# One signal per tile from TensorE and a hand-written loop, in a kernel that packs the lower triangles of 2,048 Gram matrices

## What is computed

```python
Z = jnp.einsum('bnd,bmd->bnm', inputs, inputs)      # inputs: (2048, 64, 256) float32
li, lj = jnp.tril_indices(64, k=-1)
return Z[:, li, lj]                                 # (2048, 2016) float32
```

## Time and profile before

| | us |
|---|---|
| median of 3 runs (lowest, highest) | 411.94 (411.42, 413.04) |
| the profiled execution's own time | 411.66 |
| its span, from the first to the last instruction | 409.9 |
| PE busy (matmuls) | 378.6 |
| DVE busy | 367.1 |
| ACT busy | 177.5 |
| POOL busy | 197.7 |

### The profile page before, as it was taken

One profiled execution on the slowest core, in us unless ns is written; L12 is line 12 of the kernel. 1 busy time (PEld: TensorE's weight loads), 2 busy tenths in 40 slices (PEclk: granted clock), 3 DMA queues, 4 the chain that ended last, 5 costly groups with the idle time before them and its releaser, 6 DMA issues.

```text
span 409.9 us, 68720 instructions
## 1 busy us (share of the span) xinstructions
PE 378.6 (92%) x33024; PEld 371.8 (91%) x33024; DVE 367.1 (90%) x240; ACT 177.5 (43%) x821; POOL 197.7 (48%) x974
## 2 busy tenths in 40 slices
PE   4589999999999999999999999999999999999950
PEld 4588999999999999999999999999999999999950
DVE  3328999999999999999999999999999999999965
ACT  0101245444455444555444546434555443555184
POOL 1000074663818274472818366381827457281845
PEclk9999999999999999999999999999999999999995
DMA  7259999999999999999999999999999999995407
GB/s 307 66 211 426 423 421 421 421 422 421 418 425 422 423 421 422 421 422 422 420 414 367 423 383 399 406 395 423 383 422 365 421 398 423 404 374 238 119 20 202
DMA packets 21291, 151.01 MB, mean 368 GB/s; under 512 B 2705, under 2 KB 2833, under 8 KB 4881
## 3 DMA queue, kind: packets, MB, share of 16 engines
q1 hardware_dynamic: 18752, 135.77, 82.1%
q10 hardware_dynamic: 2512, 14.97, 9.5%
HBM read 134.22 MB, written 16.52 MB: 368 GB/s over the span
## 4 chain that ended last, share of the span: by engine, by line
PE 88%; issue 4%; DVE 3%; ACTq 2%; ACT 1%; DMA 1%; DVEq 0%
PE bank_set L297 88%; ACTq L154 2%; DMA x_in<-x_dram 1%; DVE packed_rows L147 1%; DVE x_in L248 1%; DVE x_turned L224 1%; ACT products L324 1%; ACT packed_rows L142 1%; ACT packed_rows L136 0%; DVE packed_rows L136 0%; DVE x_turned L253 0%; DVEq L76 0%; DVEq L223 0%; ACTq L315 0%; DVEq L273 0%
## 5 line engine op out<-in xcount | busy, mean ns | idle before, releaser
L297 PE MATMUL bank_set<-x_turned 32*64 32x64 f32 x33024 | 378.6, 236 | 18.0 <-issue 9.1
L297 PEld LDWEIGHTS bank_set<-x_turned 32*64 32x64 f32 x33024 | 371.8, 132 | 24.7 <-issue 20.4
L224 DVE STREAM_TRANSPOSE x_turned<-x_in 128x2048 f32<-128x2048 f32 x128 | 293.1, 2293 | 33.2 <-DMA x_in<-x_dram 21.1
L147 POOL COPY packed_rows<-row_halves 32x32 f32<-32x32 f32 (+30 forms) x930 | 190.1, 204 | 202.1 <-DVE row_halves L241 164.5
L324 ACT COPY products<-bank_set 128x512 f32<-128x512 f32 (+1 forms) x91 | 68.5, 759 | 189.0 <-PE bank_set L297 170.9
L241 DVE STREAM_TRANSPOSE row_halves<-products 128x1024 f32<-128x1024 f32 x60 | 72.2, 1204 | 0.0
L142 ACT COPY packed_rows<-row_halves 128x128 f32<-128x128 f32 x240 | 53.5, 299 | 19.7 <-issue 19.0
L136 ACT COPY packed_rows<-row_halves 128x32 f32<-128x32 f32 (+30 forms) x465 | 60.8, 219 | 0.2 <-DVE row_halves L241 0.2
L324 ACT ACT_TABLE_LOAD x1 | 1.3, 1283 | 17.4 <-PE bank_set L297 17.4
L248 DVE STREAM_TRANSPOSE x_in<-products 128x512 f32<-128x512 f32 (+1 forms) x5 | 4.8, 999 | 4.0 <-ACT products L324 4.0
L147 POOL COPY packed_rows<-x_in 32x32 f32<-32x32 f32 (+30 forms) x31 | 4.9, 209 | 4.4 <-DVE x_in L248 4.4
## 6 DMA issues: line engine op xcount, KB each, us to landing
x_in<-x_dram SPq DMA_DIRECT2D x128, 1024.0 KB, 17.1
y_dram<-packed_rows ACTq DMA_DIRECT2D x21, 504.0 KB, 8.9
y_dram<-packed_rows ACTq DMA_DIRECT2D x7, 252.0 KB
y_dram<-packed_rows ACTq DMA_DIRECT2D x28, 63.0 KB
y_dram<-packed_rows SPq DMA_DIRECT2D x2, 504.0 KB, 4.8
y_dram<-packed_rows SPq DMA_DIRECT2D x1, 380.0 KB
y_dram<-packed_rows ACTq DMA_DIRECT2D x1, 380.0 KB
y_dram<-packed_rows SPq DMA_DIRECT2D x1, 124.0 KB
```

The costliest lines, as they stand in the source:

```text
L147: return copy(packed_rows[first:first + BLOCK, group % 2, :, at + BLOCK:at + i], halves(group)[first + BLOCK:first + HALF, i, :, 0:i - BLOCK])
L224: nc.vector.transpose(x_turned[:, j].rearrange("p c b s (h u n v) -> p u v (c b s h) n", h=ROWS // BLOCK, u=PAIRS, v=PAIR), x_in[:, k]).th ...
L297: done = nc.tensor.matmul(bank_sets[s][side * HALF:(side + 1) * HALF, g, at, :].rearrange("r (n u v) -> r u n v", u=PAIRS, v=PAIR), rows, ...
```

## The change

There are four edits, all about semaphores and PE's loop; no matmul, copy or DMA is added or taken away.

1. Only the last of an input tile's 128 matmuls raises `tile_multiplied[j]`, by one. `ARRAY_TILES` goes away, and the three waits on it (SP's for the late loads, DVE's, ACT's) count tiles instead of array tiles.
2. The loop of PE is written out with a register, `count`, a label, and a branch at the lap's end.
3. The register is raised by 3 in the middle of the lap's last tile (after its first slot) instead of at the lap's end.
4. Since the wait on `kept[0]` in the lap's last tile now comes behind that addition, `kept[0]` starts at 3 like `kept[1]`, and the waits of DVE on `kept[s]` are raised to match.

```diff
-    ARRAY_TILES = QUADRANTS * SIDES
...
-                    sync.wait_ge(tile_multiplied[j], (lap + 1) * ARRAY_TILES)
+                    sync.wait_ge(tile_multiplied[j], lap + 1)
...
-            pool.sem_inc(kept[1], LAP)
+            for s in range(SETS):
+                pool.sem_inc(kept[s], LAP)
...
-                    dve.wait_ge(tile_multiplied[j], lap * ARRAY_TILES)
+                    dve.wait_ge(tile_multiplied[j], lap)
...
-                    dve.wait_ge(kept[s], (lap + 1 + s) * LAP)
+                    dve.wait_ge(kept[s], (lap + 2) * LAP)
...
-            def multiply(j, step):
-
-                pe.wait_ge(turned[j], step)
+
+            count = nc.alloc_register(pe.engine, "count")
+
+            def multiply(j):
+
+                pe.wait_ge(turned[j], count)
                 s, in_set = set_of(j)
                 for slot in range(SLOTS):
                     at = in_set * SLOTS + slot
+                    if j == LAP - 1 and slot == SLOTS - 1:
+                        pe.reg_add(count, count, LAP)
                     for c in range(CHUNKS):
                         if in_set == SET_TILES[s] - 1 and slot == SLOTS - 1 and c == CHUNKS - 2:
 
-                            pe.wait_ge(kept[1 - s], step)
+                            pe.wait_ge(kept[1 - s], count)
...
-                                if c == CHUNKS - 1 and slot == SLOTS - 1:
-                                    done.then_inc(tile_multiplied[j], 1)
-
-            with pe.Fori(LAP, (LAPS + 1) * LAP, LAP) as step:
+
+                done.then_inc(tile_multiplied[j], 1)
+
+            pe.reg_mov(count, LAP)
+            pe.br("lap")
+            with nc.body("lap", valid_engines=[pe.engine]):
                 for j in range(LAP):
-                    multiply(j, step)
+                    multiply(j)
+                pe.br_lt(count, (LAPS + 1) * LAP, on_true="lap", on_false="laps_done")
+            nc.switch_bb("laps_done")
...
-                act.wait_ge(tile_multiplied[j + SET_TILES[s] - 1], (lap + 1) * ARRAY_TILES)
+                act.wait_ge(tile_multiplied[j + SET_TILES[s] - 1], lap + 1)
```

## The result

The changed kernel takes 409.09 us (median of 6 runs, 408.41 to 409.84), the kernel before 412.42 us beside it (6 runs, 411.42 to 413.65). The ratio is 0.9919, with a 95% interval of 0.9896 to 0.9942: 3.3 us faster, where 3.4 us were forecast. By the interval the gain lies between 2.4 and 4.3 us. The profiled execution of the changed kernel took 408.65 us, with a span of 406.9 us against 409.9 us.

What follows compares the result with a forecast made beforehand. PE and the DMA engines were taken to bound the kernel at one pace within 1%. Tile 122 3.1 us earlier, tile 123's end another 0.2, the start about 0.1: 3.4 us off 411.94, so 408.5 us, range 406.4 to 410.6 us.

Steps and rivals of the forecast that it cites:

- two resources at one pace: In mid-kernel a group of eight tiles costs the DMA engines 23.6 us and PE 23.4 us, the same within 1%.
- The signals: At each tile's end inside a lap, one signal for eight saves PE 0.12 us, 0.24 us per lap.
- the met wait in mid-tile: Near the middle tile's end, PE's already met wait on `kept[1]` costs nothing: 84 records, where the ordinary pace gives 85.
- The loop: At PE's lap end only the branch remains; the addition and the move go, 0.065 us less per lap.
- laps between the stores of 8.4 to 8.5 us: Sign to look for in PE's timeline after the change: laps between stores should take 8.4 to 8.5 us.
- DVE would not stop PE: In mid-kernel DVE is busy 8.43 us a lap, just under PE's new 8.475 us.
- The last store's delay: Behind the last delaying store PE begins tile 122 at 374.7 us, between 374.5 and 374.9 us, 3.1 us earlier.
- The tail keeps its length: From tile 123's end ACT is the chain; the tail keeps its length and moves by 3.3 us.
- my first rival: At the end group 13's stores issue faster and PE becomes the chain: 4 to 5 us earlier, about 407 us; chance 0.14.
- The addition in mid-tile: Rival: in the lap's last tile it empties PE's queue, stopping PE 0.35 us per lap: 413.8 us; chance 0.05.
- The second rival: At tile ends, in the loop or in the stores' DMA costs the gain is lost: 410.5 to 412 us; chance 0.17.
- The fourth rival: PE's clock falls to 1.2 GHz in pauses behind stores, adding 28 us: 430 us or more; chance 0.02.

Runs made afterwards that it cites:

- the addition at the end: Changed kernel with the register's addition back at the lap's end, just ahead of the branch: 409.71 us, ratio 0.9938 to the kernel before.
- the single signal alone: Kernel before plus one signal per tile in place of eight, old loop kept: 409.28 us, ratio 0.9920.
- the written-out loop alone: Kernel before plus the written-out loop with the addition in mid-tile, eight signals kept: 410.36 us, ratio 0.9939.
- the two cuts: DVE turns half of each tile from tile 6, groups 0 to 12 store 16 columns: before 411.1 us, whole change 391.8 us.
- small stores and an early load 4: Changed kernel with six stores for groups 0 to 12, two for group 13, load 4 not held back: 415.00 us, ratio 1.0064.
- the early load 4: Changed kernel with load 4 no longer held back until tile 1 is multiplied: 404.71 us, ratio 0.9806 to the kernel before.

## Why the prediction was right, step by step

**The step that carried it: two resources at one pace.** The landing of load 122 at 372.0 us was forecast not to move, and it did not, while PE's own lap fell by half a microsecond. The gain is PE's distance behind the loads, and no more. What the prediction calls the pace of the DMA engines is the pace of the few that are furthest behind. Its 3.7 us for a group's stores is a measured difference and already contains that, so the sum was not harmed.

**The signals.** The share of the tile's end was right (0.14 us counted); what I took off was 0.12 us each, and all of it went, 0.145 us. That the met wait in mid-tile costs nothing was the right ground for it.

**The loop: the term that was mis-sized.** I took off 0.065 us, the recorded 36 and 29 ns. It was 0.17 us. The step that failed is reading a sequencer instruction's record as its cost. At the lap's end each of the two costs 0.08 to 0.10 us. With both terms PE's own lap is 8.28 us, not 8.475 us, so the sign "laps between the stores of 8.4 to 8.5 us" did not come. That the total came out nearly right in spite of it is owed to the cap, which hides PE's pace: 0.2 us a lap over 40 laps is 8 us that never reached the end.

**DVE would not stop PE.** Only just. Three laps of the changed kernel before the loads become the limit take 24.79 us, 8.26 us each (length, busy of PE, PEld, DVE, ACT, POOL, clock, DMA share, GB/s):

```profile
59.78:84.57 24.79, 24.79 (x2311) 24.58 (x2305) 24.79 (x14) 12.47 (x56) 14.94 (x75) 1.00 1.01 421
```

DVE is busy in all of it. Its limit is thus 8.26 us a lap; my 8.43 us, from its busy time before, was too high. A turn behind a wait takes 2.31 us, two turns without one 4.46 us together (both in the timeline below), and in the kernel before more of the turns stood behind a wait. PE and DVE now run side by side at one pace. None of this decided anything, since the loads' pace is 8.83 us.

**The last store's delay.** The forecast was that tile 121 waits and tile 122 follows, at 374.7 us between my two cases. What happened, in the timeline of the changed kernel:

```profile
369.61 2.31 DVE L224 STREAM_TRANSPOSE x_turned<-x_in 128x2048 f32<-128x2048 f32 x1 [1.63 <-DMA x_in<-x_dram]
371.84 1.20 DVE L241 STREAM_TRANSPOSE row_halves<-products 128x1024 f32<-128x1024 f32 x1
371.97 2.95 PE L302 MATMUL bank_set<-x_turned 32*64 32x64 f32 x256 [0.99 <-DVE x_turned L224]
372.97 4.46 DVE L224 STREAM_TRANSPOSE x_turned<-x_in 128x2048 f32<-128x2048 f32 x2
375.29 13.71 PE L302 MATMUL bank_set<-x_turned 32*64 32x64 f32 x1248 [0.37 <-DVE x_turned L224]
```

Tile 121 did wait for its load. But between the two turns DVE had 1.20 us of row turning to do, so tile 122 was turned late and PE began it at 375.29 us: 2.5 us earlier than before, not 3.1 us. I had left out what stands between the two on DVE's queue. The sum of 3.4 us for the span was too high by this; it came out at 3.0 us. That the medians differ by 3.3 us, closer to the forecast, is luck, since their interval is wider than the difference.

**The tail keeps its length.** It did: ACT's copy of tile 123 begins at 381.05 us instead of 383.89 us, 2.84 us earlier, and the six stores cost ACT 6.97 us again, so my first rival did not come about.

```profile
381.05 1.01 ACT L333 COPY products<-bank_set 128x1024 f32<-128x1024 f32 x1 [1.90 <-PE bank_set L302]
381.12 6.97 ACTq L153 DMA_DIRECT2D y_dram<-packed_rows  x6
```

From that copy to the end it is 25.85 us, against 26.0 us before.

**The other rivals.** The addition in mid-tile does not empty PE's queue: the full change's lap is shorter than that with the addition at the end. The second rival, no effect, is outside the interval.

The fourth rival, the clock, did not come in the changed kernel, whose pauses behind the stores are at most 1.2 us. But the prediction held it to be small because of one trace, and other runs show more. In the trace of the single signal alone the granted clock was at the 1.2 GHz level from 8.6 to 29.1 us, after a first pause like that in the trace of before, and so it was in the written-out loop alone and in the whole change, both with the two cuts (pauses of 3.35 and 3.70 us). This is the clock row of the first of these traces, where a 5 stands for half of the full clock:

```profile
PEclk9559999999999999999999999999999999999995
```

And in the kernel with small stores and an early load 4 it fell in mid-kernel, after a pause of PE of 1.60 us behind a late tile. The rows are that stretch and the one behind it (length, busy, records, clock, DMA share, GB/s):

```profile
257.10:260.40 3.30, 3.30 (x247) 0.50 0.92 348
260.60:263.90 3.30, 3.30 (x314) 1.00 0.91 298
```

That cost 67 records, or 0.7 us, once. The laps compared above, from 100 to 360 us, all had the full clock.

## What to carry to other kernels

When an engine is to be made faster, first measure the pace of every resource that it shares the beat with, the loads above all: here PE and the DMA engines were within 1%, and 19 us of PE's time turned into 3.3. What is left after that is the engine's distance behind the next limit at the last place where that limit bites, and the further gain lies in moving that limit, as with the early load 4. And a cost should be counted as records that did not begin in a stretch, not as the duration of the sequencer instruction that stands there. When transfers are the limit, look at how many of the DMA engines still work while the last loads land: a full DMA share in mid-kernel can hide that one to five of them set the pace.

## What the runs showed of the hardware

- Eight signals from matmuls of eight array tiles at a tile's end cost PE 0.145 us more than one signal does; at a lap's end, where PE stops for the branch anyway, they cost nothing that shows (0.25 us between the weight loads of two laps with eight signals or one).
- On PE's sequencer, register instructions recorded with 29 and 36 ns cost 0.10 and 0.08 us ahead of or behind a branch. The same 36 ns addition in mid-tile costs nothing that shows (1.98 us for the 188 records around it, with or without it).
- With only a branch of 208 ns left at the lap's end, 176 matmul records begin in the 2.0 us around it instead of 189, so it costs about 0.14 us.
- Stores in two DMAs of 504 KB or in six from 504 to 63 KB hold up the loads differently, and not by their sizes alone: alternating the two forms by group is faster than either form throughout (409.1, 416.2 and 419.5 us, the last with group 13 in two DMAs). Why is open.
- A load has landed when the last of its 16 steps has come, and stores can leave a few of these far behind: one by 17.2 us with large stores alone, four by 9.7 to 15.7 us with small ones, five by 9.9 to 16.4 us with both in turn, none by more than 0.2 us with next to no stores.
- The same first pause of PE (3.35 to 3.70 us) is followed by the 2.4 GHz level in some executions and by the 1.2 GHz level, until about 29 us, in others. In one run the granted clock fell to 1.2 GHz for a few us after a pause of 1.60 us.
- PE's code, fetched in the first lap, comes later when loads are in flight: the last stop for it grew from 1.57 to 4.86 us.
